# Gate logits of the first layer with the gate matrix as weights, four transposes, and one selection for two batches

## What is computed

```python
H = jax.nn.gelu(xf @ W1 + b1, approximate=False)          # 64 -> 256
probs = jax.nn.softmax((H @ Wg + bg) / TEMP, axis=-1)     # 256 -> 8 gate logits
assign = jnp.argmax(probs, axis=-1)
out = jnp.zeros_like(xf)
for e in range(Wd.shape[0]):                              # 8 experts
    y = H @ Wd[e] + bd[e]                                 # 256 -> 64
    sel = (assign == e)[:, None]
    out = out + jnp.where(sel, probs[:, e:e + 1] * y, 0.0)
```

## Time and profile before

| | |
|---|---|
| time, median of 3 runs | 5362.7 us (5359.76 to 5366.95) |
| the profiled execution | 5365.49 us, its span 5363.8 us |
| mean granted TensorE clock of the span | 0.936 of full speed |
| loop of the first layer | 7 rounds of 105.75 us |
| the gate products of batch 0 and of batch 1, in one round | 4.47 + 6.83 us |

### The profile page before, as it was taken

One profiled execution on the slowest core, in us unless ns is written; L12 is line 12 of the kernel. 1 busy time (PEld: TensorE's weight loads), 2 busy tenths in 40 slices (PEclk: granted clock), 3 DMA queues, 4 the chain that ended last, 5 costly groups with the idle time before them and its releaser, 6 DMA issues. The chain is left out here.

```text
span 5363.8 us, 122278 instructions
## 1 busy us (share of the span) xinstructions
PE 4898.8 (91%) x41817; PEld 2236.0 (42%) x41847; DVE 3805.6 (71%) x6984; ACT 3162.5 (59%) x3388; POOL 2187.5 (41%) x2110
## 2 busy tenths in 40 slices
PE   5888887999999999999999979999999999999965
PEld 3444443333333333333333334444444444444433
DVE  5566665666666666666666658888888888888878
ACT  1222221566666666666666627777777777777754
POOL 2122214333333332333333325665565556565556
PEclk8878878899999999999999969999999999999976
DMA  4111110000000000000000000000000000000001
GB/s 109 32 47 31 47 31 0 1 2 2 2 2 2 2 2 2 2 2 1 2 2 2 1 1 2 3 3 3 3 3 2 3 3 3 3 2 3 3 5 28
DMA packets 43526, 52.90 MB, mean 10 GB/s; under 512 B 33164, under 2 KB 33295, under 8 KB 42896
## 3 DMA queue, kind: packets, MB, share of 16 engines
q1 hardware_dynamic: 39160, 44.34, 3.2%
q10 hardware_dynamic: 3736, 0.38, 0.1%
HBM read 39.70 MB, written 4.19 MB: 8 GB/s over the span
## 5 line engine op out<-in xcount | busy, mean ns | idle before, releaser
L1553 DVE TENSOR_REDUCE a_mp<-psum 128x1 f32<-128x512 f32 x2072 | 1324.3, 685 | 684.5 <-PE psum L1430 677.2
L2218 DVE TENSOR_REDUCE f_mp<-psum 128x1 f32<-128x512 f32 (+2 forms) x2614 | 1344.2, 574 | 197.4 <-PE psum L2066 144.8
L2016 ACT ACTIVATE f_prob<-psum,escale_f 128x1024 f32<-128x1024 f32 x1152 | 1241.8, 1112 | 278.4 <-PE psum L2134 147.4
L1398 ACT ACTIVATE a_prob<-psum,escale 128x1024 f32<-128x1024 f32 x1024 | 1087.8, 1111 | 536.0 <-PE psum L1479 535.8
L1487 PE MATMUL psum<-a_prob,a_v 128*64 128x512 f32 x4104 | 997.5, 607 | 0.0
L2056 PE MATMUL psum<-f_kf,f_qf 64*128 64x512 f16 (+3 forms) x3138 | 674.2, 332 | 54.6 <-DVE f_mp L2218 50.0
L1904 POOL TENSOR_SCALAR f_hi<-f_raw,part 128x512 f16<-128x512 f32 x320 | 501.0, 1566 | 486.4 <-ACT f_raw L1981 486.4
L2147 PE MATMUL psum<-f_prob,f_vh 128*32 128x512 f32 (+3 forms) x6144 | 614.7, 495 | 3.1
L1318 POOL TENSOR_TENSOR a_u<-a_og,a_inv 128x512 f32<-128x512 f32 x129 | 134.6, 1043 | 1165.8 <-DVE a_inv L1568 1165.8
L2126 PE MATMUL psum<-f_qf,f_kf 64*128 64x512 f16 (+3 forms) x3074 | 512.2, 329 | 31.1 <-issue 12.0
L1487 PEld LDWEIGHTS psum<-a_prob,a_v 128*64 128x64 f32 x4104 | 249.7, 136 | 507.4 <-issue 502.1
(11 more groups left out here) (425 smaller groups left out, 7331.0 us busy)
## 6 DMA issues: line engine op xcount, KB each, us to landing
idx<-in_itok_BS_dram SPq DMA_DIRECT2D x36, 512.0 KB, 6.2
idx<-in_itok_BS_dram SPq DMA_DIRECT2D x54, 256.0 KB, 7.3
idx<-in_x_dram SPq DMA_DIRECT2D x18, 256.0 KB, 3.8
a_qh<-a_rowT SPq DMA_DIRECT2D x258, 1.0 KB
out_dram<-h SPq DMA_DIRECT2D x16, 256.0 KB, 2.6
f_qf<-f_rowT SPq DMA_DIRECT2D x130, 4.0 KB, 1.8
wd<-in_L_ffn_Wd_dram SPq DMA_DIRECT2D x2, 256.0 KB
aw<-in_L_attn_WQ_dram SPq DMA_DIRECT2D x2, 128.0 KB
```

The lines of the kernel that those rows point to most:

```text
L1398: act.activation(prob[:, part], k.psum[:, pair:pair + 2].rearrange("p b n -> p (b n)"), ACT.Exp, scale=k.escale[:]).then_inc(s.read, 1)
L1553: dve.tensor_reduce(mp[:, tg % 2, t + 4 * r, c:c + 1], bank_of(j + r), X, ALU.max)\
L2016: act.activation(prob[:, u % NPF], k.psum[:, pair:pair + 2], ACT.Exp, scale=k.escale_f[:])\
L2218: ins = dve.tensor_reduce(side[:, at:at + 1], bank_of(j + r)[:, col:col + nk], X, ALU.max)
```

## The change

The operands of the gate product are exchanged. `wg` (128 by 8) becomes the weights, and 512 tokens of `hT` stream. The result has the experts on the partitions: batch j and half of the tokens at partitions 32 x (2j + half) to + 8 of bank 6, all four groups in one bank. ScalarE copies the whole bank to a new tile `gT` (`gates`), TensorE turns it by four 128 x 128 transposes into bank 7 (`gates_turn`), and VectorE's `chosen` and `weighed` then run once over both batches, with 128 numbers on each partition where there were 64. The exponential is also one instruction.

```diff
+                def gates(pair):                       # ScalarE
+                    done("gate", pair * 2 + 2)
+                    act.activation(gT[:], ps[6], ACT.Copy).then_inc(E["gT"], 1)
...
+                    if n == 1 and front is None:
+                        gates(back)
                     for j in range(2):
...
                         if n == 1:
                             deviation(j, "var1", "sd1", b)
+                            if j == 0 and back is not None:
+                                gates(back)
...
                     if n == 2 and back is not None:
-                        for j in range(2):
-                            done("lg", back * 2 + j + 1)
-                            act.activation(eg[:, j], lg[:, j], ACT.Exp).then_inc(E["eg"], 1)
+                        done("lg", back + 1)
+                        act.activation(eg[:], lg[:], ACT.Exp).then_inc(E["eg"], 1)
...
                 def gate(pair, j):                     # TensorE
                     done("gelu", pair * 4 + 2 + j + 1)
-                    for t in range(T):
-                        for c in range(2):
-                            last = pe.matmul(ps[6 + j][:, t * EXPERTS:(t + 1) * EXPERTS], lhsT=hT[:, j, c, t * P:(t + 1) * P],
-                                             rhs=k.wg[:, c], start=(c == 0 and t == 0), stop=(c == 1), skip_group_check=True)
+                    for c in range(2):
+                        for half in range(2):
+                            at = 32 * (2 * j + half)
+                            last = pe.matmul(ps[6][at:at + EXPERTS], lhsT=k.wg[:, c],
+                                             rhs=hT[:, j, c, half * HALF:(half + 1) * HALF],
+                                             start=(c == 0), stop=(c == 1), skip_group_check=True)
                     last.then_inc(E["gate"], 1)
+
+                def gates_turn(pair):
+                    done("gT", pair + 1)
+                    for t in range(4):
+                        last = pe.transpose(ps[7][:, t * P:(t + 1) * P], gT[:, t * P:(t + 1) * P], k.ident[:])
+                    last.then_inc(E["gturn"], 1)
...
                 def experts(pair, n):
-                    if n < 2:
-                        done("lg", pair * 2 + n + 1)
+                    if n == 0:
+                        done("gT", pair + 1)
+                    elif n == 1:
+                        done("lg", pair + 1)
...
+                    if n == 2 and back is not None:
+                        gates_turn(back)
...
-                def chosen(link, pair, j):             # VectorE
+                def chosen(link, pair):
-                    w, l, g = wsel[:, j], lg[:, j], g1[:, j]
-                    done("gate", b + 1)
-                    link(dve.tensor_tensor(l, ps[6 + j][:, 0:T * EXPERTS].rearrange("p (t e) -> p t e", t=T),
-                                           rows(k.bg[:], T), ALU.add))
+                    w, l = wsel[:].rearrange("p j t e -> p (j t) e"), lg[:].rearrange("p j t e -> p (j t) e")
+                    done("gturn", pair + 1)
+                    link(dve.tensor_tensor(lg[:].rearrange("p j (a t) e -> p (j a) t e", a=2),
+                                           ps[7].rearrange("p (t q x) -> p q t x", t=4, x=32)[:, :, :, 0:EXPERTS],
+                                           k.bg[:].unsqueeze(1).unsqueeze(1).to_broadcast([P, 4, 4, EXPERTS]), ALU.add))
...
-                        for j in range(2):
-                            if n == 1:
-                                chosen(link, back, j)
-                            if n == 2:
-                                weighed(link, back, j)
+                        if n == 1:
+                            chosen(link, back)
+                        if n == 2:
+                            weighed(link, back)
```

More of the change, by code:

```diff
@@ L610 @@
             "vx", "kf", "qf", "ctx", "cx", "num", "den", "aT", "proj", "x2", "cen3", "sq3", "var3", "sd3", "xn3",
-            "hid", "gelu", "gate", "lg", "eg", "wsel", "tr", "xt", "y", "y_taken", "pt", "tree", "h", "var4", "sd4")
+            "hid", "gelu", "gate", "lg", "eg", "tr", "xt", "y", "y_taken", "pt", "tree", "h", "var4", "sd4", "gT", "gturn")
 class Link:
@@ L656, in layer0 @@
         eg = sb("l0_eg", [P, 2, T, EXPERTS], F32)
-        g1 = sb("l0_g1", [P, 2, 4, T], F32)
+        g1 = sb("l0_g1", [P, 4, 2 * T], F32)
+        gT = sb("l0_gT", [P, HALF], F32)
         wsel = sb("l0_wsel", [P, 2, T, EXPERTS], F32)
@@ L974, in scaled @@
                     return dve.tensor_tensor(out, ps[j], rs[:, j], ALU.mult)
-                def chosen(link, pair, j):
-                    b = pair * 2 + j
-                    w, l, g = wsel[:, j], lg[:, j], g1[:, j]
-                    done("gate", b + 1)
-                    link(dve.tensor_tensor(l, ps[6 + j][:, 0:T * EXPERTS].rearrange("p (t e) -> p t e", t=T),
-                                           rows(k.bg[:], T), ALU.add))
-                    link(dve.tensor_reduce(g[:, 0], l, X, ALU.max))
-                    link(dve.tensor_tensor(w, l, wide(g[:, 0], EXPERTS), ALU.is_equal))
-                    dve.tensor_tensor(l, l, wide(g[:, 0], EXPERTS), ALU.subtract).then_inc(E["lg"], 1)
-                    link(dve.tensor_tensor(w, w, rows(k.rank[:], T), ALU.mult))
-                    link(dve.tensor_reduce(g[:, 1], w, X, ALU.max))
-                    link(dve.tensor_tensor(w, w, wide(g[:, 1], EXPERTS), ALU.is_equal))
@@ L990, in weighed @@
-                def weighed(link, pair, j):
-                    b = pair * 2 + j
-                    w, e, g = wsel[:, j], eg[:, j], g1[:, j]
-                    done("eg", b + 1)
-                    link(dve.tensor_reduce(g[:, 2], e, X, ALU.add))
-                    link(dve.reciprocal(g[:, 3], g[:, 2]))
-                    link(dve.tensor_tensor(e, e, wide(g[:, 3], EXPERTS), ALU.mult))
+                def chosen(link, pair):
[4 more added lines that the diff above has]
+                                           k.bg[:].unsqueeze(1).unsqueeze(1).to_broadcast([P, 4, 4, EXPERTS]), ALU.add))
+                    link(dve.tensor_reduce(g1[:, 0], l, X, ALU.max))
+                    link(dve.tensor_tensor(w, l, wide(g1[:, 0], EXPERTS), ALU.is_equal))
+                    dve.tensor_tensor(l, l, wide(g1[:, 0], EXPERTS), ALU.subtract).then_inc(E["lg"], 1)
+                    link(dve.tensor_tensor(w, w, rows(k.rank[:], 2 * T), ALU.mult))
+                    link(dve.tensor_reduce(g1[:, 1], w, X, ALU.max))
+                    link(dve.tensor_tensor(w, w, wide(g1[:, 1], EXPERTS), ALU.is_equal))
@@ L998, in weighed @@
+                def weighed(link, pair):
+                    w, e = wsel[:].rearrange("p j t e -> p (j t) e"), eg[:].rearrange("p j t e -> p (j t) e")
+                    done("eg", pair + 1)
+                    link(dve.tensor_reduce(g1[:, 2], e, X, ALU.add))
+                    link(dve.reciprocal(g1[:, 3], g1[:, 2]))
+                    link(dve.tensor_tensor(e, e, wide(g1[:, 3], EXPERTS), ALU.mult))
                     link(dve.tensor_tensor(w, w, e, ALU.mult))
@@ L1082, in _ @@
                 start = link.n
-                steps = start + 28
+                steps = start + 18
                 with dve.Fori(0, PAIRS_ - 1) as i:
```

## The result

The changed kernel takes 5286.7 us (median of 4 runs, 5281.1 to 5292.5) where the kernel before takes 5361.2 (4 runs, 5351.6 to 5367.0): ratio 0.9863, interval 0.9845 to 0.9881.

What follows compares the result with a forecast made beforehand. A chain of waits through both gate blocks in slots 0 to 2 bounds each round; 7.9 us a round, 55.3 over seven, plus 4.1 behind the loop, gives 59.4 us: 5303.3 us median, range 5288 to 5333.

Steps and rivals of the forecast that it cites:

- Gates: Gate product of a batch in the first layer's loop: 8 rows for 32, 1.9 us at clock 1.00.
- Chain of slots 0 to 2: Gates, variance, root, reciprocal, centring of the front pair: batch 0 gains 3.4 us, centring of batch 1 7.25 a round.
- Copy and transposes: ScalarE's copy (0.59 us) and TensorE's four transposes (0.8 us): free while VectorE's 9.4 us of reciprocal work cover them.
- `weighed`: Selection step on the path ahead of slot 3's reciprocal: 4 instructions instead of 8, gain 0.7 us a round.
- The rest of the round ... Later slots shift as a whole: After centring of batch 1: nothing changes up to the exponential, clock still at half, and later slots only shift.
- The term behind the loop: Last pair's gates, copy and transposes ahead of its experts: 7.3 us for 11.45, gain 4.1 us.
- upper case: Round gains more, since centring and transposes behind may run at full clock: up to 2 us a round, 5289; chance 0.06.
- No overlap: Rival: gate rows do not overlap but keep full clock; gain 6.0 us a round, 5320 us; chance 0.12.
- half clock: Rival: gates overlap but the clock still falls in them; gain 4.1 us a round, 5332 us; chance 0.12.
- slower: Rival: neither overlap nor full clock, gates 7.5 us a batch; 3.4 us a round lost, 5391 us; chance 0.04.
- given back: Rival: another anchor, the ids' transfer or the experts' buffers, sets the round; 5363 us; chance 0.04.
- A change of form: Switching TensorE's tiling form: three or four further changes a round cost nothing, at most 2 us in all.

Runs made afterwards that it cites:

- the doubled ones: Changed kernel with the copy of bank 6 and each of the four transposes made twice: 5285.6 us, ratio 0.9850.
- Filled in slot 7 alone: Kernel before plus 9 bf16 products of constants, result unread, between the two products of slot 7: 5336.2 us, ratio 0.9956.
- selection: Kernel before with only `chosen`, `weighed` and the exponential merged over both batches: 5329.2 us, ratio 0.9947.
- even by more (21.0): Kernel before plus one unread VectorE multiplication of constants (0.7 us) a round behind `weighed`: 5349.9 us, ratio 0.9984.
- filled changed kernel: Changed kernel plus unread TensorE products of constants ahead of both centrings, the projections and the last expert: 5321.0 us, ratio 0.9926.
- two kernels filled alike: Kernel before and changed kernel, each with unread TensorE products of constants in slots 2, 4 and 9: 5339.6 and 5321.0 us.

## Why the prediction was right and wrong

**Gates.** Right: 1.89 us a batch for 1.9, clock at 1.00. The prediction took 1.00 because the new rows stream 512 columns as those ahead of the gates do. The runs bear that out as far as they go: rows of 64 columns with the old weight loads kept 1.00 too, where rows of 8 had lost it.

**Chain of slots 0 to 2.** Right: 4.8 us for 4.5 in slots 1 to 3; from the first gate row to the first reciprocal 3.70 us for 7.14 before, a gain of 3.4 as forecast. That slots 9 to 1 as a whole gave 3.6 a round is in part luck, since single rounds gave 3.0 to 5.2 with the clock. What was forecast next came too: VectorE was late, with its reciprocals 4.57 us apart for 4.7. Copy and transposes cost nothing, as the doubled ones show. `weighed` at 0.8 for 0.7.

**The step that failed: "The rest of the round ... Later slots shift as a whole".** The mechanism of the change was right, and this term, booked at 0, was mis-sized: slots 3 to 9 gave 8.9 us over the loop. The term behind the loop was too small as well, 7.7 us for 4.1; gates, copy and transposes gave 6.3 of it, and the experts behind them 1.6. The other stretches come to 1.3 us more than forecast, and the layer to 73.3 for 59.4. What the step overlooked is that TensorE's speed in later slots is no constant of those slots: the half clock behind the wait in slot 7 (3.4 us in every round of the kernel before) and the one soon behind slot 3 (10.2 us in all but the first) were read as part of the kernel and carried over. Filled in slot 7 alone, the kernel before loses 26.2 us of its layer, and it is moved out of the pattern by less work (selection, 26.1) and in its profile even by more (21.0).

The trace of the kernel before had a sign of it. Its first round was 2.7 us shorter than the others, 2.3 of it in slots 3 to 9, which the reading "all seven take the same 105.75 us" passed over. An estimate of the upper case from that trace alone: 2.3 us in the six other rounds, and in all seven the loss in slot 7, which is 1.3 us by 4 rows of 3.20 for 1.88 and 0.4 by the product ahead of them (1.55 for 1.12). That is 26 us more, and the low end at some 5278 instead of 5288. The prediction did give 0.06 to a larger gain, but by another way, the centring and transposes in slot 2 at full clock. That did not come: those of batch 1 still took 2.07 and 1.91 us at 0.50. The filled changed kernel shows what they are worth, 1.0 us a round.

**The rivals.** No overlap, half clock, slower and given back did not come. A change of form showed no price: the first variance starts 1.82 us after the gates' first row (431.93 to 433.75), 0.07 us before they end. The Trainium skill, TensorEngine Tiling (Array Packing), section Key Properties, says that the array drains there; if so, it is within these numbers. Sixteen gate rows over four column groups took 1.90 us, as 8 did over two (1.89): they overlap, though all use the same rows of the array. The Trainium skill, TensorE: Matmul & The Clock Gate, section The mechanism, says that weight loads overlap running products only where row groups differ. The trace does not agree for these loads of 8 columns (0.09 us each): the third pair of them starts at 432.36, while the rows that began at 431.93 run to 432.52 by the profile, and both use all rows.

**What stays open.** I could not say beforehand which pattern a round falls into; it repeats from execution to execution in the changed kernel (725.7 to 725.8 us in three profiles, one of them with the loops of the gates exchanged) but moved with 0.7 us of added work. What lengthened the attention loop of the filled changed kernel by 33 us is open too. How much of the 73.3 us would be left without any loss of clock on either side was not measured; two kernels filled alike differ by 51.9, in which each still loses it in places.

## What to carry to other kernels

Here products of 8 streaming columns behind 128-column weight loads went with a fall of TensorE's clock, and what came behind paid too: before exchanging operands it is worth trying whether more streaming columns alone, even of zeros, are faster (59 us here). When the rounds of a loop have the same length to 0.1 us and a granted clock well below 1 (0.81 here), look where the clock falls in them, and read the one round that differs, since an edit may end or bring such a pattern. Give a forecast an extra case for it, and judge edits by stretches between fixed events, not by the total. Short fillers in one wait of TensorE gave 26 us in the kernel before and 14 in the changed one, but with more of them, in other places, the program lost 33 us in a loop that nobody had touched.

## What the runs showed that I had not expected

Added VectorE work made the kernel before faster (5349.9 us for 5358.7). Streaming 64 columns was faster than streaming 8 with the same weights (3.68 us for 6.83 in the second block). The loop order of the products did not change how column groups overlap (1.90 and 1.89 us). And 51 more products in one loop went along with a later loop that is 33 us longer, while 50 more in the kernel before did not.
